# Pairwise attention pooling: each logit half cut in two column parts, one part behind every z duo

## The reference

```python
row, col = np.triu_indices(F, k=1)          # 741 pairs
ip = x[:, row, :] * x[:, col, :]
hidden = jax.nn.relu(jnp.einsum('bpd,da->bpa', ip, W_w) + b_w)
logits = jnp.einsum('bpa,a->bp', hidden, W_h) + b_h[0]
a = jax.nn.softmax(logits, axis=1)[:, :, None]
pooled = jnp.sum(a * ip, axis=1)
return pooled @ W_p + b_p
```

## Time and profile before

| | us |
|---|---|
| median of 3 runs | 1224.09 (1223.74 to 1224.36) |
| the profiled execution | 1223.86 |
| its span, first to last instruction | 1222.1 |
| TensorE busy | 1177.5 (96%), 29440 matmul records |
| of it z duos (L420) | 834.6, 16384 records |
| of it logit halves (L439) | 442.3, 8192 records |
| VectorE, ScalarE, GpSimd busy | 1014.1, 931.1, 479.1 |
| mean granted TensorE clock | 0.993 |

### The profile page before, as it was taken

How to read it: one execution, slowest core, us unless ns; L and a number is a source line. 1 busy time by engine, 2 the same in 40 slices (tenths; PEclk the granted TensorE clock), 3 DMA queues, 4 the chain that set the end, 5 groups by cost and what they waited for, 6 DMA issues and landing times.

```text
span 1222.1 us, 68735 instructions
## 1 busy us (share of the span) xinstructions
PE 1177.5 (96%) x29440; PEld 525.3 (43%) x29440; DVE 1014.1 (83%) x741; ACT 931.1 (76%) x1185; POOL 479.1 (39%) x262
## 2 busy tenths in 40 slices
PE   6899999999999999999999999999999999999994
PEld 2444444444444444444444444444444444444441
DVE  6878889888887988888888888988888888888861
ACT  4677778778777777777777777777777777777763
POOL 1243434434344443434434344444434434344230
PEclk9999999999999999999999999999999999999997
DMA  1112131211313113131221413113131231313102
GB/s 39 37 34 42 36 44 34 45 38 30 43 40 43 30 40 43 31 47 35 40 41 32 43 39 37 38 39 44 30 48 35 39 40 33 43 38 45 32 16 20
DMA packets 255133, 45.85 MB, mean 38 GB/s; under 512 B 255073, under 2 KB 255073, under 8 KB 255073
## 3 DMA queue, kind: packets, MB, share of 16 engines
q1 hardware_dynamic: 255072, 45.17, 23.0%
HBM read 26.59 MB, written 18.54 MB: 37 GB/s over the span
## 4 chain that ended last, share of the span: by engine, by line
PE 93%; issue 3%; ACT 1%; DVE 1%; SPq 1%; DMA 0%; ACTq 0%; DVEq 0%
PE z L420 57%; PE logits L439 27%; PE cross L397 5%; PE cross L386 4%; ACT hidden L349 1%; ACT exps L357 0%; DVE prod L264 0%; PE logits L430 0%; DMA bp_col<-in_L_rec_b_p_dram 0%; SPq L177 0%; SPq L174 0%; SPq L145 0%; SPq L180 0%; SPq L179 0%; DVE gram_out L273 0%
## 5 line engine op out<-in xcount | busy, mean ns | idle before, releaser
L349 ACT ACTIVATE hidden<-z,b_col 128x742 f32<-128x742 f32 x1024 | 860.2, 878 | 262.3 <-PE z L420 261.8
L264 DVE TENSOR_TENSOR prod<-x_wide 128x2964 f32<-128x2964 f32 x256 | 829.1, 3245 | 128.1 <-PE z L420 127.2
L420 PE MATMUL z<-prod,w_tiles 64*32 64x370 f32 (+1 forms) x16384 | 834.6, 478 | 10.9 <-DMA bp_col<-in_L_rec_b_p_dram 7.7
L227 POOL COPY head_w<-head_cols 128x64 f32<-128x64 f32 x252 | 477.7, 1896 | 699.6 <-PE logits L439 699.6
L439 PE MATMUL logits<-hidden,head_w 64*32 64x371 f32 (+1 forms) x8192 | 442.3, 473 | 8.7 <-issue 8.0
L420 PEld LDWEIGHTS z<-prod,w_tiles 64*32 64x32 f32 x16384 | 243.0, 105 | 415.9 <-issue 385.9
L439 PEld LDWEIGHTS logits<-hidden,head_w 64*32 64x32 f32 x8192 | 175.2, 106 | 156.9 <-issue 59.9
L273 DVE COPY gram_out<-cross 103x464 f32<-103x464 f32 x128 | 80.6, 630 | 3.4 <-PE cross L397 3.4
L397 PE MATMUL cross<-x_wide,x_scaled 64*39 64x58 f32 x4096 | 79.5, 215 | 2.4 <-issue 2.4
L386 PEld LDWEIGHTS cross<-ident,x_rows 78*128 78x128 f32 x512 | 43.6, 142 | 82.1 <-issue 78.4
L342 ACT ACTIVATE x_scaled<-x_wide,wp_col 128x312 f32<-128x312 f32 x128 | 69.9, 546 | 7.1 <-DMA bp_col<-in_L_rec_b_p_dram 7.1
(11 more groups left out here) (16 smaller groups left out, 14.6 us busy)
## 6 DMA issues: line engine op xcount, KB each, us to landing
x_rows<-in_r_x_dram SPq DMA_DIRECT2D x256, 78.0 KB
gram<-gram_out SPq DMA_DIRECT2D x512, 35.3 KB
values<-gram SPq DMA_DIRECT2D x128, 46.3 KB, 3.5
out_dram<-y_all SPq DMA_DIRECT2D x8, 1.0 KB, 3.5
w_tiles<-in_L_rec_W_w_dram SPq DMA_DIRECT2D x4, 16.0 KB, 2.1
head_cols<-in_L_rec_W_h_dram SPq DMA_DIRECT2D x4, 0.2 KB, 2.3
b_col<-in_L_rec_b_w_dram SPq DMA_DIRECT2D x2, 0.2 KB, 2.3
wp_col<-in_L_rec_W_p_dram SPq DMA_DIRECT2D x2, 0.2 KB, 2.3
```

What stands on the lines that cost most here:

```text
L227: nc.gpsimd.tensor_copy(head_w[:, step % AHEAD, :, :], head_cols[:, :, at:at + TILE]).then_inc(head_w_ready, 1)
L264: nc.vector.tensor_tensor(prod[:, (2 * slot + half) % AHEAD, :, :].rearrange("p q (i k) -> p q i k", k=OFFSETS), one, other, ALU.mult).the ...
L349: nc.scalar.activation(hidden[:, e, q, :, :], z[:, q % 2, :, 0:HCOLS], ACT.Relu, bias=b_col[:, 0:1]).then_inc(hidden_ready, 1)
L420: last = nc.tensor.matmul(z[col:col + TILE, q % 2, b, 0:cols.stop - cols.start], w_tiles[row:row + D, col:col + TILE], prod[row:row + D, e ...
```

## The change

`logit_half` becomes `logit_quarter`, which takes a column range: columns 0 to 185, or 186 to 370. The first and second quarter are the first half's two column parts, the third and fourth the second half's. Each quarter has as many matmuls as a half had (8, so 16 records and as many weight loads), over half of the columns. In `body` one quarter stands ahead of each z duo: first, z3, second, z0, third, z1, (cross work), fourth, z2. The semaphores move with them: half_done is raised by the second quarter and waited for by the third, logits_done by the fourth. The second and fourth quarter have no wait.

```diff
-            def logit_half(e, half):
+            def logit_quarter(e, half, cols):
 
                 for q in range(QUADS):
                     for c in range(2):
                         b, row = half ^ c, c * A
-                        last = nc.tensor.matmul(logits[TILE * q:TILE * (q + 1), b, 0:HCOLS - b],
-                                                head_w[row:row + A, e, b, :],
-                                                hidden[row:row + A, e, q, b, 0:HCOLS - b],
+                        own = slice(cols.start, min(cols.stop, HCOLS - b))
+                        last = nc.tensor.matmul(logits[TILE * q:TILE * (q + 1), b, own],
+                                                head_w[row:row + A, e, b, :], hidden[row:row + A, e, q, b, own],
                                                 start=False, stop=True, skip_group_check=True,
                                                 tile_position=(row, TILE * q))
                 return last
 
-            def first_half(step, e):
+            QUARTERS = (slice(0, HCOLS // 2 + 1), slice(HCOLS // 2 + 1, HCOLS))
+
+            def first_quarter(step, e):
                 pe.wait_ge(head_w_ready, step + 1)
                 pe.wait_ge(hidden_ready, QUADS * (step + 1))
                 if not (isinstance(step, int) and step == 0):
                     pe.wait_ge(logits_done, step)
                 nc.tensor.sem_inc(z_claimed, 1)
-                logit_half(e, 0).then_inc(half_done, 1)
-
-            def second_half(step, e):
+                logit_quarter(e, 0, QUARTERS[0])
+
+            def second_quarter(e):
+                logit_quarter(e, 0, QUARTERS[1]).then_inc(half_done, 1)
+
+            def third_quarter(step, e):
                 pe.wait_ge(half_done, step + 1)
                 nc.tensor.sem_inc(z_claimed, 1)
-                logit_half(e, 1).then_inc(logits_done, 1)
+                logit_quarter(e, 1, QUARTERS[0])
+
+            def fourth_quarter(e):
+                logit_quarter(e, 1, QUARTERS[1]).then_inc(logits_done, 1)
 
             def body(k, with_x=True):
                 for e in range(AHEAD):
                     step = AHEAD * k + e
-                    first_half(step, e)
+                    first_quarter(step, e)
                     hidden_layer(step + 1, (e + 1) % AHEAD, 3)
+                    second_quarter(e)
                     hidden_layer(step + 2, (e + 2) % AHEAD, 0)
-                    second_half(step, e)
+                    third_quarter(step, e)
                     hidden_layer(step + 2, (e + 2) % AHEAD, 1)
                     if e % 2 == 1:
                         cross_work(2 * k + 1 + e // 2, e // 2, k + 3, with_x)
+                    fourth_quarter(e)
                     hidden_layer(step + 2, (e + 2) % AHEAD, 2)
...
-            first_half(step + 2, 2)
-            hidden_layer(step + 3, 3, 3)
-            second_half(step + 2, 2)
-            first_half(step + 3, 3)
-            second_half(step + 3, 3)
+            for e in range(2, 4):
+                first_quarter(step + e, e)
+                if e == 2:
+                    hidden_layer(step + 3, 3, 3)
+                second_quarter(e)
+                third_quarter(step + e, e)
+                fourth_quarter(e)
```

More of the change, by code:

```diff
@@ L502, in _ @@
             for e in range(2):
-                first_half(step + e, e)
+                first_quarter(step + e, e)
                 hidden_layer(step + e + 1, e + 1, 3)
+                second_quarter(e)
                 hidden_layer(step + e + 2, e + 2, 0)
-                second_half(step + e, e)
+                third_quarter(step + e, e)
                 hidden_layer(step + e + 2, e + 2, 1)
+                fourth_quarter(e)
                 hidden_layer(step + e + 2, e + 2, 2)
-            first_half(step + 2, 2)
-            hidden_layer(step + 3, 3, 3)
-            second_half(step + 2, 2)
-            first_half(step + 3, 3)
-            second_half(step + 3, 3)
+            for e in range(2, 4):
+                first_quarter(step + e, e)
+                if e == 2:
+                    hidden_layer(step + 3, 3, 3)
+                second_quarter(e)
+                third_quarter(step + e, e)
+                fourth_quarter(e)
 _INS = ['r_x', 'L0_rec_W_w', 'L0_rec_b_w', 'L0_rec_W_h', 'L0_rec_b_h', 'L0_rec_W_p', 'L0_rec_b_p']
```

## The result

The changed kernel takes 1247.7 us (median of 4 runs, 1246.13 to 1248.23) against 1224.22 of the kernel before beside it: ratio 1.0188, 95% interval 1.017 to 1.0206. It is 23.5 us slower; 1249 was forecast. The profiled execution took 1246.13 us, with a span of 1244.4.

The account below looks back on a forecast made before the run. The z buffers' round trip of 1.98 us, not TensorE's work, was taken to bound the steady steps. 1223.9 - 10 (steps) + 25.5 (group ends) + 4 (code) + 6 (clock) = 1249 us, range 1230 to 1272.

Parts of the forecast that it names:

- Term 1: Steady steps: the z buffers' 1.98 us round trip still binds, quarters take 0.31 us; -10 us, between -12 and +2.
- the step on the jump: Pair of steps with the loop's jump: the fourth quarter covers most of 0.12 us, leaving 0.04; 9.01 against 9.16 us.
- Term 2: End of a group: softmax chain starts behind the cross work, 2.58 us lost instead of 0.88; +25.5 us over 15 groups.
- Term 3: Added instructions: about 6 more packets of instruction queue to fetch at 0.7 us each; +4 us, between 0 and 8.
- Term 4: Group ends: longer TensorE idle lets the clock drop to half behind some openings; +6 us, between 0 and +25.
- The share of a quarter: Group ends: a quarter of the 15 idle stretches taken to be followed by a clock drop; +6 us.
- (a): Steady steps: TensorE's work sets the pace, round trip shrinks with even spacing, pairs cost 1.87 us; 1207 us, chance 0.09.
- (b): Group ends: the softmax stays hidden as before by a delay the steps win back; about 1218 us, chance 0.04.
- (c): Logit quarters: short matmuls bound by their count, a quarter costs a half's 0.62 us; about 1520 us, chance 0.04.
- (d): Loop code: the longer loop no longer stays loaded and is fetched anew each pass; +200 us, chance 0.03.

Follow-up runs that it names:

- the short rectification: ScalarE rectifies only the first of each duo's two column parts: 1167.8 us on the kernel before, 1211.8 us on the changed kernel.
- the split kernel: The kernel before with each half issued as two quarters, one right behind the other, in the old places: 1218.8 us, ratio 0.9962.
- the kernel of 1217 us: The changed kernel with the fourth quarter right behind the third in the last step of each block of four: 1217.0 us, ratio 0.9946.

## Why the prediction was right, point by point

The time, its sign and its mechanism came out as forecast, 1.3 us off. By terms the agreement is less tight, and that it is so close is luck: errors of 3, 6, 2 and 2 us largely cancel.

*Term 1, the steady steps*: forecast 8.97 and 9.01, measured 8.97 and 9.07. The round trip binds, at 1.98; the short rectification shows it. What failed is the step on the jump: I left 0.04 of stall at it, but the first quarter comes 0.70 behind z2 (610.36 to 611.06), not 0.62 to 0.66, and moves z3, z1 and all behind them. Against 8.99 and some 9.16 before, a group gains 4 x 0.02 + 4 x 0.09 = 0.44 us, 16 groups 7 us rather than 10.

*Term 2, a group's end*: forecast 2.58 us for the changed kernel against 0.88. Measured 11.75 - 9.07 = 2.68 against 10.03 - 9.16 = 0.87, so +1.81 x 15 = +27 rather than +25.5. The missed 0.1 is one link: I took the exp's wait behind the bias (618.38 to 618.55) for the end of a rectification, which would be gone. Nothing is ahead of the exp now, and it still starts 0.17 behind (629.67 + 0.27 to 630.11). It is the way from VectorE to ScalarE. My own term also lumped the opening's 0.6 us in with the softmax; since both kernels have it, the difference was right.

*Term 3, more code*: this step failed. The packets of the instruction queue rose from 22 to 28, the six that I had counted, but at no price of 0.7 us each. The span grew by 22.3 us (1222.1 to 1244.4). Between the third opening and the last one it grew by 22.1 (955.0 to 977.1). What is left, 0.2, has to hold two more ends of groups and the steps of three more groups, 2 x 1.81 - 3 x 0.44 = 2.3 us. So the start and the end got some 2.1 us cheaper, not 4 dearer; the split kernel shows the same sign with nothing moved. 1.7 of the 2.1 is the clock drop at 1182 us, to which nothing answers in the changed kernel. Dividing stall time by packets was the error: it charges the mean of an uneven cost to the next unit. What sets that cost stays open.

*Term 4, the clock*: 3 drops, in groups of 76.43, 76.15 and 76.08 us against 74.85, so 1.2 to 1.6 us each and 4.1 together; I had 6 and bounds from 0 to 25. The share of a quarter was a guess from one stretch of two, and that it came near is luck: with the same idle 3, 6 and 11 of 15 openings were followed by a drop, in different kernels.

Sum by measured terms: -7.0 + 27.2 - 2.1 + 4.1 = 22.2, against 22.3 in the spans. The forecast's 25.5 had term 1 too good by 3, term 3 too dear by 6, term 4 too dear by 2, and term 2 too cheap by 1.7. The profiled execution is also the shortest of the four; against the median the growth is 23.5. In the recorded working 12 x 0.62 is 7.44 and 2 x (0.62 + 0.31) is 1.86, not 7.46 and 1.87; nothing hangs on it.

The rivals: (a) needed a round trip below 1.93, and it stayed at 1.98. (b) is out, the idle ahead of the openings is 2.00 us. (c) is out, a quarter takes 0.31. (d) is out: the middle of the run keeps its pace, and from 150 to 1130 us no packet of q8 moves in the changed kernel either.

## What to carry to other kernels

When a producer and a consumer alternate over two buffers, add up one buffer's round trip (fill, wake, drain, wake) before believing a busy share of 96%: work put ahead of a waiting item is free there, and the same work moved behind an item that doesn't wait costs its full length. When work is spread out to even a stream, ask what its **last** piece releases: here each piece was as cheap as hoped, but the final one set off a serial chain of 2.4 us across two engines, once a group. The steps' gain can be kept by an exception at that one place: of the 7 us of the kernel of 1217 us, 2.6 are shown to be such a gain, and the rest may be the start's and the end's.

## What the runs showed of the hardware that was not expected

GpSimd's copy of head_w (L227, 128x64) took 1.90 us on average before and 0.87 after, with nothing changed in it. In the kernel before it stands under VectorE's product; GpSimd's timeline and VectorE's:

```profile
595.04 1.95 POOL L227 COPY head_w<-head_cols 128x64 f32<-128x64 f32 x1 [3.04 <-PE logits L439]
```

```profile
593.64 3.25 DVE L264 TENSOR_TENSOR prod<-x_wide 128x2964 f32<-128x2964 f32 x1 [0.58 <-PE z L420]
```

It ends at 596.99, 0.10 behind the product's end at 596.89. In the changed kernel one that starts while VectorE copies from PSUM takes 0.24:

```profile
619.77 0.24 POOL L227 COPY head_w<-head_cols 128x64 f32<-128x64 f32 x1 [4.07 <-PE logits L440]
```

It is not one case: of the 252 copies 220 begin under a product in the kernel before, and 206 of them end 0.09 to 0.10 us behind it, the other 14 as much behind the next product. So the copy stood still until the product was over, and the later logits_done moved many copies out from under one: 129 still begin there. It costs nothing here, since head_w is wanted three steps later. The Trainium skill says of this (SBUF — State Buffer, "SBUF: two separate sides") that VectorE and GpSimd share a port pair under an exclusive lock, and that a VectorE operation with two SBUF inputs, if it starts first, keeps out a GpSimd operation that reads SBUF for the whole instruction; the trace agrees, with these ends 0.09 to 0.10 us behind the product's.

Idle stretches of 2.00 us at the same place of the same loop (1.78 at the last opening) are followed by the lower clock in some groups and not in others: 3 of 15 in the changed kernel, 3 in it with the 128 more instructions, 6 with the short rectification and 11 with the late half unsplit. And the parts where code runs for the first time did not get longer with more instructions in them: the last stretch is 88.3 us in the kernel before, 83.7 with the halves split, and 86.9 with the halves split and shifted. Why is not shown.
